# Attention stage: the q/k product in the second block behind the bonus turn, its turn at the third block's end, the rotation in the fourth, and a contiguous tile for the bonus

## What is computed

```
x  = layernorm(input)
Q  = normalize(x @ W_q.T)          # 16 heads of 4 values
K  = normalize(x @ W_k.T)
V  = x @ W_v.T                     # 16 heads of 64 values
Qn = normalize(Q rotated per head by W_nudge)
s  = sigmoid(3 * K @ simple_roots.T)
k_bonus = per head, a table of 16 bonuses mixed by products of s and 1 - s
scores  = Qn @ K.T / 2 + k_bonus over the keys, causal mask
out     = softmax(scores) @ V @ W_out.T
result  = input + layernorm(out)
```

## Time and profile before

| | before |
|---|---|
| median of 3 runs | 1770.89 us (1768.71 to 1771.26) |
| the profiled execution | 1770.72 us, its span 1769.0 us |
| PE busy | 1650.8 us, 93% of the span |
| DVE, ACT, POOL busy | 1317.2, 889.0, 1000.8 us |
| attention layer | to about 772 us of the span |
| one round in the loop | 22.29 us |

### The profile page before, as it was taken

One profiled execution on the slowest core, in us unless ns is written; L12 is line 12 of the kernel. 1 busy time (PEld: TensorE's weight loads), 2 busy tenths in 40 slices (PEclk: granted clock), 3 DMA queues, 4 the chain that ended last, 5 costly groups with the idle time before them and its releaser, 6 DMA issues.

```text
span 1769.0 us, 47120 instructions
## 1 busy us (share of the span) xinstructions
PE 1650.8 (93%) x14871; PEld 1237.2 (70%) x14871; DVE 1317.2 (74%) x3869; ACT 889.0 (50%) x2003; POOL 1000.8 (57%) x1782
## 2 busy tenths in 40 slices
PE   5999999999999999849999999999999999789996
PEld 3677777777777777537788888777787886555553
DVE  5588888888888888745567777777777775748886
ACT  2666666666666666514444444444444442224443
POOL 7788888888888888712223333333333333227777
PEclk9999999999999999969999999999999999689998
DMA  1011111111111113010110000000000002434441
GB/s 42 11 50 55 51 49 50 50 49 51 53 54 54 54 54 104 14 36 25 60 60 31 31 31 31 22 30 23 28 30 29 25 25 99 155 116 134 134 131 41
DMA packets 78259, 95.96 MB, mean 54 GB/s; under 512 B 7046, under 2 KB 62995, under 8 KB 78160
## 3 DMA queue, kind: packets, MB, share of 16 engines
q1 hardware_dynamic: 70992, 77.91, 13.9%
q0 software_dynamic: 7168, 16.87, 2.7%
HBM read 53.14 MB, written 43.69 MB: 55 GB/s over the span
## 4 chain that ended last, share of the span: by engine, by line
PE 39%; DVE 8%; issue 5%; POOL 2%; DMA 1%; ACT 1%; DVEq 0%; POOLq 0%; SPq 0%; ACTq 0%
PE main L1371 6%; PE main L1373 5%; PE main L1380 5%; PE main L1529 3%; PE yp L1451 3%; PE main L1311 2%; PE xi L1286 2%; PE main L1435 2%; PE main L1324 2%; PE main L1438 1%; PE main L1436 1%; PE route L1543 1%; PE xi L1543 1%; PE turn L1279 1%; POOL out L1269 1%
## 5 line engine op out<-in xcount | busy, mean ns | idle before, releaser
L662 ACT ACTIVATE wgu<-score 128x384 f32<-128x384 f32 x512 | 223.2, 490 | 80.2 <-PE score L484 78.8
L1371 PE MATMUL main<-hT_high,h_high 128*128 128x512 f32 x512 | 221.2, 432 | 0.9 <-ACT hT_high L1628 0.9
L1373 PE MATMUL main<-hT_high,h_low 128*128 128x512 f32 x512 | 201.3, 393 | 0.0
L506 PE MATMUL outp<-wgu 128*32 128x256 f32 (+1 forms) x4096 | 196.3, 333 | 3.3 <-POOL wgu L327 2.2
L327 POOL TENSOR_SCALAR_AFFINE_SELECT wgu<-wgu 128x512 f32<-128x512 f32 x256 | 166.4, 655 | 52.0 <-ACT wgu L662 34.3
L506 PEld LDWEIGHTS outp<-wgu 128*32 128x32 f32 x4096 | 116.6, 111 | 69.5 <-issue 23.3
L1380 PE MATMUL main<-hT_low,h_high 128*128 128x512 f32 x512 | 138.3, 391 | 0.1
L1936 DVE SCALAR_TENSOR_TENSOR th<-th,main 128x512 f32<-128x512 f32 x64 | 43.9, 685 | 115.2 <-ACT th L1655 115.2
L544 PE MATMUL back<-wout,wgu 128*128 128x128 f32 x1024 | 128.6, 280 | 0.0
L544 PEld LDWEIGHTS back<-wout,wgu 128*128 128x128 f32 x1024 | 121.8, 195 | 0.4
L1269 POOL DMA_INDIRECT out<-res,idx x96 | 96.7, 1008 | 44.3 <-issue 40.7
(11 more groups left out here) (295 smaller groups left out, 4361.4 us busy)
## 6 DMA issues: line engine op xcount, KB each, us to landing
sorted_d<-row_buf SPq DMA_DIRECT2D x26, 772.0 KB, 3.7
xg<-sorted_d SPq DMA_DIRECT2D x48, 386.0 KB
wgu<-in_gate_up SPq DMA_DIRECT2D x4, 2048.0 KB
xa<-in_x SPq DMA_DIRECT2D x32, 128.0 KB, 3.4
xr<-in_x SPq DMA_DIRECT2D x32, 128.0 KB, 3.2
x_d<-x SPq DMA_DIRECT2D x32, 128.0 KB, 1.8
x1c<-x_d SPq DMA_DIRECT2D x16, 256.0 KB, 2.8
x1v<-x_d SPq DMA_DIRECT2D x16, 256.0 KB, 2.7
```

Source lines behind the costliest of these rows:

```text
L506: m = pe.matmul(outp[AUG * j:AUG * (j + 1), p % 2, k * P:T], val[par][:, k, h, v:v + AUG], weights(h, k), start=(k == 0), stop=(k == 1), t ...
L662: act.activation(prob[:, h // 2 % (RING // 2), :, h % 2, :], score[h % BANKS][:, 0:SC].rearrange("p (c q) -> p c q", q=P), ACT.Exp).then_i ...
L1371: pe.matmul(main[m % 2][:, :], w[0][:, k, m * P:(m + 1) * P], src[0][:, k, :], start=(k == 0), stop=False)
L1373: pe.matmul(main[m % 2][:, :], w[1][:, k, m * P:(m + 1) * P], src[0][:, k, :], start=False, stop=False)
```

## The change

The q/k product of `n` moves on PE from block one to block two, behind the bonus turn. The turn of `qkn` moves from the start of block three's products to their end, behind the k turn. The rotation moves from there to block four, behind the fourth `spread_out`. On ACT the square, the copy of the turned q/k values and the three reads of the rotated values move to fit. On DVE `first_sums` and `roots` move from ahead of the first `normalise` to behind the running maximum, and `scaled` from behind the first `normalise` to behind the last write of `q5`.

The bonus goes into a tile of its own, `bonus_row`, of one value per row, from which the bonus turn reads its weights contiguously. POOL copies it from there to the last column of `k5_wide` with one more instruction, which the split of `k5` waits for (`bon_k`). One constant is cleared once.

```diff
@@ bonus, on POOL
-                        else k5_wide[:, 0:TT * HEADS, DH:DH + 1]
+                        else bonus_row[:, 0:TT * HEADS].rearrange("p (r o) -> p r o", o=1)
                     did(pool.tensor_tensor(out, t, pair[:, :, :, 0], ALU.add))
+                    if r == 3:
+                        pool.tensor_scalar(k5_wide[:, 0:TT * HEADS, DH], bonus_row[:, 0:TT * HEADS], 1.0, 0.0,
+                                           ALU.mult, ALU.add).then_inc(s["bon_k"], 1)
@@ step, on PE
                 values(f, par, 0)
-                if n is not None:
-                    wait(pe, s["xnT"], n + 1)
-                    for i in range(TT):
-                        mm = pe.matmul(front[:, T + i * P:T + (i + 1) * P], xnT[par][:, i * P:(i + 1) * P], wqk[:],
-                                       start=True, stop=True)
-                    mm.then_inc(s["p_qk"], 1)
                 scores(b, par, 2)
                 weighted(b, par, 0)
                 scores(b, par, 3)
                 values(f, par, 1)
                 spread_out(z, 0)
                 if f is not None:
                     wait(pe, s["bon"], BON * (f + 1))
                     wait(pe, s["qaT"], f)
                     for i in range(TT):
-                        mm = pe.matmul(turned[:, i * P:(i + 1) * P], k5_wide[:, i * HEADS:i * HEADS + P, DH], ident[:],
+                        mm = pe.matmul(turned[:, i * P:(i + 1) * P], bonus_row[:, i * HEADS:i * HEADS + P], ident[:],
                                        start=True, stop=True)
                     mm.then_inc(s["p_bonT"], 1)
+                if n is not None:
+                    wait(pe, s["xnT"], n + 1)
+                    for i in range(TT):
+                        mm = pe.matmul(front[:, T + i * P:T + (i + 1) * P], xnT[par][:, i * P:(i + 1) * P], wqk[:],
+                                       start=True, stop=True)
+                    mm.then_inc(s["p_qk"], 1)
                 values(f, par, 2)
@@ step, on DVE
-                first_sums(n)
-                roots(n, f)
                 normalise(z, par, 0)
-                scaled(n)
                 if f is not None:
                     wait(dve, s["p_bonT"], f + 1)
                     dve.tensor_copy(bonT[:], turned[0:HEADS, 0:T]).then_inc(s["bonT"], 1)
...
                     dve.tensor_tensor_scan(out=cmax[0:HEADS, :], data0=bonT[:], data1=bonT[:], initial=bonT[:, 0:1],
                                            op0=ALU.max, op1=ALU.max).then_inc(s["cmax"], 1)
+                first_sums(n)
+                roots(n, f)
                 normalise(z, par, 1)
...
                                       -1.0, None, ALU.mult).then_inc(s["q5"], 1)
+                scaled(n)
                 normalise(z, par, 2)
```

More of the change, by code:

```diff
@@ L158, in attention_layer @@
         bonT = sb("bonT", [HEADS, T])
+        bonus_row = sb("bonus_row", [P, P + HEADS])
         cmax = sb("cmax", [P, T])
@@ L206, in attention_layer @@
         N_IDENT = 4
-        N_CONST = 22
+        N_CONST = 23
         ctx.callback(clear, nc, list(s.values()))
@@ L295, in late_constants @@
                 const(pool.memset(k5_wide[:], 0.0))
+                const(pool.memset(bonus_row[:], 0.0))
                 const(pool.memset(cmax[:], 0.0))
@@ L420, in step @@
                     wait_apart(pool, s["kcopy"], f + 1, s["const"])
+                    wait_apart(pool, s["bon_k"], f + 1, s["const"])
                     wait_apart(pool, s["p_kaT"], f, s["const"])
@@ L587, in step @@
                 values(f, par, 0)
-                if n is not None:
-                    if isinstance(n, int) and n == 0:
-                        pe.wait_ge(s["w_qk"], 32)
-                    wait(pe, s["xnT"], n + 1)
-                    for i in range(TT):
-                        mm = pe.matmul(front[:, T + i * P:T + (i + 1) * P], xnT[par][:, i * P:(i + 1) * P], wqk[:],
-                                       start=True, stop=True)
-                    mm.then_inc(s["p_qk"], 1)
                 scores(b, par, 2)
@@ L606, in step @@
                     for i in range(TT):
-                        mm = pe.matmul(turned[:, i * P:(i + 1) * P], k5_wide[:, i * HEADS:i * HEADS + P, DH], ident[:],
+                        mm = pe.matmul(turned[:, i * P:(i + 1) * P], bonus_row[:, i * HEADS:i * HEADS + P], ident[:],
                                        start=True, stop=True)
                     mm.then_inc(s["p_bonT"], 1)
+                if n is not None:
+                    if isinstance(n, int) and n == 0:
+                        pe.wait_ge(s["w_qk"], 32)
+                    wait(pe, s["xnT"], n + 1)
[3 more added lines that the diff above has]
+                    mm.then_inc(s["p_qk"], 1)
                 values(f, par, 2)
@@ L616, in step @@
                 spread_out(z, 1)
-                if n is not None:
-                    wait(pe, s["qkn"], n + 1)
-                    for i in range(TT):
-                        mm = pe.transpose(front[:, i * P:(i + 1) * P], qkn[:, i].rearrange("p h c -> p (h c)"),
-                                          ident[:])
-                    mm.then_inc(s["p_qkT"], 1)
                 values(f, par, 3)
@@ L630, in step @@
                 spread_out(z, 2)
+                if f is not None:
+                    wait(pe, s["q5"], f + 1)
+                    turn_operands(k_aug, "k", f)
+                if n is not None:
+                    wait(pe, s["qkn"], n + 1)
+                    for i in range(TT):
+                        mm = pe.transpose(front[:, i * P:(i + 1) * P], qkn[:, i].rearrange("p h c -> p (h c)"),
+                                          ident[:])
+                    mm.then_inc(s["p_qkT"], 1)
+                scores(b, par, 6)
+                weighted(b, par, 2)
+                scores(b, par, 7)
+                spread_out(z, 3)
                 if n is not None:
@@ L636, in step @@
                     mm.then_inc(s["p_rot"], 1)
-                if f is not None:
-                    wait(pe, s["q5"], f + 1)
-                    turn_operands(k_aug, "k", f)
-                scores(b, par, 6)
-                weighted(b, par, 2)
-                scores(b, par, 7)
-                spread_out(z, 3)
                 output(z, par, range(0, 5))
@@ L692, in step @@
                 copy_values(f, par, 0)
-                if n is not None:
-                    wait(act, s["p_qk"], n + 1)
-                    wait(act, s["ss1"], n)
-                    act.activation(sq1[:].rearrange("p r c -> p (r c)"), front[:, T:2 * T],
-                                   ACT.Square).then_inc(s["sq1"], 1)
                 weights(b, 4, 5)
@@ L705, in step @@
                 copy_values(f, par, 1)
+                if n is not None:
+                    wait(act, s["p_qk"], n + 1)
+                    wait(act, s["ss1"], n)
+                    act.activation(sq1[:].rearrange("p r c -> p (r c)"), front[:, T:2 * T],
+                                   ACT.Square).then_inc(s["sq1"], 1)
                 copy_values(f, par, 2)
@@ L710, in step @@
                 weights(b, 10, 11)
+                copy_values(f, par, 3)
+                weights(b, 12, 13)
                 if n is not None:
@@ L713, in step @@
                     act.activation(qkT[:], front[:, 0:T], ACT.Copy).then_inc(s["qkT"], 1)
-                copy_values(f, par, 3)
-                weights(b, 12, 13)
+                copy_out(b, par, 2)
+                weights(b, 14, 15)
                 if n is not None:
@@ L723, in step @@
                     act.activation(qraw[:], fr[:, :, 0], ACT.Copy).then_inc(s["qraw"], 1)
-                copy_out(b, par, 2)
-                weights(b, 14, 15)
                 if f is not None:
```

2 lines of the change are left out of this document (1 added, 1 removed).

## The result

The changed kernel takes 1861.44 us (median of 4 runs, 1855.18 to 1864.68), the one before 1769.80 us (median of 4) on the same chip. The ratio is 1.0514, 95% interval 1.0488 to 1.0539: 92 us slower. The forecast was slower, 1823 us with a range of 1797 to 1847. The direction was right and the time lies 14 us above the range.

What follows compares the result with a forecast made beforehand. The prediction took PE, the matrix engine, to bound the kernel; new waits eat the gains, leaving 1.26 + 0.44 = 1.70 us per round, 31 rounds, 52.7 us on 1770.7: 1823 us, range 1797 to 1847.

Steps and rivals of the forecast that it cites:

- What bounds the kernel: Attention loop: PE is the bound, busy 22.12 of 22.29 us per round; no other chain may grow beyond its cover.
- (a): Bonus turn: contiguous weights bring the next work after 0.44 us instead of 0.81, a gain of 0.37 us per round.
- (b): First block: 0.88 us leaves with the q/k product, which returns in block two at 0.44; gain 0.44 us per round.
- Wait one: First block: PE stands 0.72 us before the weighted product, waiting for POOL's second mask.
- Wait two: End of third block: PE stands 1.67 us before the third spread product, waiting for DVE's second normalisation.
- from the square sums to the following normalisation: DVE chain ahead of the second normalisation: 4.51 us, taken from the old order; the normalisation adds 0.69.
- The bounds: Unknown root lengths and event-to-PE times: 0.91 us per round over 29 rounds to 2.47 over 31, 1797 to 1847 us.
- the rule on the shared port pair: DVE roots beside POOL: two-SBUF-input VectorE and GpSimd instructions take turns; borne out only in part, two thirds of nine unstretched.
- The sum: Whole loop: 1.26 us late at block four's scores plus 0.44 for the rotation, 1.70 per round, 52.7 over 31 rounds.
- Block four: Fourth block: the rotation adds 0.44 us on PE with nothing to hide it; the late ACT and DVE work adds nothing.
- rival 4: Attention loop: PE's clock falls to 0.89 through standing, 79 us more over 29 rounds, about 1902 us; chance 4%.
- the prediction's own signs of being wrong: Profile after: second normalisation waits for PE instead of PE for it, or granted clock in the loop below 1.00.

Runs made afterwards that it cites:

- the filling: Changed kernel plus 24 small TensorE products nobody reads, ahead of the running maximum's turn, before the wait for the second normalisation: 1830.37 us, ratio 1.0354.

## Why the prediction was right and wrong

**What bounds the kernel** was right: PE, with chains around it that had little slack: 0.26 us for the second mask, and 0.39 for the second normalisation, which ended at 320.35 (its line is below) where PE used it at 320.74. Every version here with a new wait in every round was slower.

```profile
319.66 0.69 DVE L817 TENSOR_TENSOR wgu<-spread,wgu 128x512 f32<-128x512 f32 x1
```

**The gains** (a) and (b) are there, as predicted (0.61 us for four records, no wait at L613), and are lost in the waits, as predicted.

**Wait one** was right: 0.72 forecast, 0.56 and 0.87 in the alternating rounds, 0.71 on average. The 0.3 between the two kinds I had not seen, since I read one round only, and in the kernel before no wait shows it. In the round from 416.13 ScalarE's first exponentials start 0.60 us after the scores, in the one from 341.25 it is 0.38, and the first mask follows them. The timeline of ScalarE at both places:

```profile
341.35 0.39 ACT L740 ACTIVATE y_sb<-back 128x256 f32<-128x256 f32 x1 [0.37 <-PE back L550]
341.63 0.87 ACT L668 ACTIVATE wgu<-score 128x384 f32<-128x384 f32 x2
...
416.24 0.38 ACT L740 ACTIVATE y_sb<-back 128x256 f32<-128x256 f32 x1 [0.37 <-PE back L550]
416.73 0.87 ACT L668 ACTIVATE wgu<-score 128x384 f32<-128x384 f32 x2
```

Both wait for the same copy, but in the second the exponentials don't overlap its end. The kernel before has the same difference, 0.39 us after the scores in its round from 306.68 and 0.60 in the one from 328.97:

```profile
307.07 0.87 ACT L662 ACTIVATE wgu<-score 128x384 f32<-128x384 f32 x2
...
329.57 0.87 ACT L662 ACTIVATE wgu<-score 128x384 f32<-128x384 f32 x2
```

Why this is so in every second round is open.

**Wait two** was right in mechanism and place and too small in size: 1.97 us against 1.67. The term that was mis-sized is "from the square sums to the following normalisation", 4.51 us. It measured 356.23 - 351.35 = 4.88. From the first sum to the first root instruction it took 0.92 us instead of 0.68, since one of the sums took 0.47 instead of 0.20: this is 0.24 of the 0.37. The rest lies in the roots, where four instructions are stretched instead of three. The bounds named the roots as an unknown and had no term for the sums; the round still lies inside them.

**Why roots are stretched.** On the rule on the shared port pair, from the Trainium skill, page "SBUF — State Buffer", the prediction said that the trace bears it out only in part, and read that from the share of time in which GpSimd is busy. What counts is what GpSimd does when the root instruction starts. In the kernel before, from 85 to 700 us, the 98 root instructions that start while GpSimd is idle all take 0.26 us, and the 56 that start inside a mask all take 0.57 or more. In the kernel after it is 48 and 48. Those that start inside other GpSimd instructions end 0.09 to 0.18 us after that instruction, and take more than 0.26 only where this makes them. So two stretched ones of the earlier trace rows stand beside masks, and not one: the second mask starts at 314.99, and the root at 315.18 took 0.57. The third, 0.43 at 316.37, starts inside another GpSimd instruction (316.09 to 316.69). The same in the round after:

```profile
354.57 0.57 DVE L771 TENSOR_TENSOR root_t<-sums,root 128x96 f32<-128x96 f32 x1
```

```profile
354.38 1.26 POOL L329 TENSOR_SCALAR_AFFINE_SELECT wgu<-wgu 128x512 f32<-128x512 f32 x2
```

This agrees with the rule of the Trainium skill in which of the root instructions are late, in both loops. The prediction had it that by this rule every root instruction that meets GpSimd would be late. But the rule makes only the one wait that starts second: the root at 313.99 in the round before, inside which the mask of 314.09 starts, took 0.26.

**The sum.** 1.70 us per round was forecast. At full clock it is 2.14: 1.99 in one kind of round and 2.28 in the other. Of the 0.44 (0.46 against the one round of 22.29 that the prediction worked from), 0.31 is the longer chain (from the weighted product to the third spread product 11.13 us instead of 10.82), and 0.08 lies between that spread product and the scores of block four (356.98 to 358.08, 1.10 us instead of 1.02; the q/k turn behind the k turn adds more than the 0.14 that it took before). The rest, 0.07, is the weighted product of the first block, which starts 4.60 or 4.90 us into the round, 4.75 on average instead of 4.68. Block four took 7.47 us, as forecast. Over 31 rounds this makes 66 us instead of 53, 1836 us, which lies inside the range.

**What failed is rival 4, the clock.** It had 4%, with the words "the waits are short and spread, which speaks against it". That step was wrong: the sum put the clock at 1.00 and its price at nothing, and the granted clock in the loop is 0.95, which costs 31 us (28 by the ratios). Without it the time would be 1830 us, inside the range. A clock below 1.00 in the loop was also one of the prediction's own signs of being wrong. The profile had a row that spoke for it, with a clock of 0.89 where PE was busy 57 of 75 us. I read it as a matter of that stretch. The rival also had its price, 79 us if the loop ran at 0.89. Looking back, the better reading would have been to take the lower clock as a likely part of the forecast, with a price of 0 to 79 us, since 2.4 us of standing per round was my own number. That it is standing that brings the clock down is shown by the filling; why it falls in some rounds and not in others with the same waits stays open.

## What to carry to other kernels

A step that is moved behind a wait of PE costs little and gives nothing (here 0.1 us a round between the two places of the q/k product); ask first what the answer to it (here the roots) now stands in front of. Where TensorE is busy 99% of the time and a change makes it stand one or two microseconds at one place in every round, the clock belongs in the forecast as a term with a price, and not among the unlikely cases. Whether a loss is the chain or the clock can be tried cheaply: fill the wait with products that nobody reads, ahead of the wait itself, and see which part of the loss goes.

## What the runs showed of the hardware that I had not expected

- How much the clock costs doesn't follow from how long TensorE stands in all. The changed kernel stands 0.71 and 1.97 us per round, at a clock of 0.95 from 85 to 700 us, and loses 31 us to it; with the product in block one it stands 2.13 us at the one place (and 0.17 at the product), at 0.89, and loses 69 us. The length of the longest wait alone doesn't order them either: with the roots early TensorE stands 2.5 and 0.7 us, at 0.91. With 0.70 and 0.55 us the clock in the loop stays at 1.00. What sets it is not shown.
- Work added to TensorE made the kernel faster: 24 products of 0.056 us, 1861 to 1830 us, and 1907 to 1838 us.
- The price of a fall of the clock is paid behind the wait. In the kernel with the product in block one the matmuls up to 398 us ran at full speed, the clock fell within the wait (0.83 on average from 398.25 to 400.38), and the matmuls from 400.38 to about 406.5 ran at half. In the changed kernel's round from 365.55 it fell later: TensorE went on from 381.60 to 383.00 at 1.00, and from there to 386.40 at 0.50.
- Rounds of one loop body with two copies of the same code can differ by 0.3 us for good, in a way that slack hides (22.29 and 22.33 before, 24.30 and 24.59 after).
- A 0.26 us VectorE instruction with two inputs in SBUF that starts inside a GpSimd mask took 0.57 us or more in all 104 cases of the two loops, and one that starts while GpSimd is idle 0.26 in all 146.
